# Masked attention stages: VectorE's minimum takes three heads of four, TensorE's penalties one, and the first unit's x leads the queue

## What is computed

```python
# stage 0 (L0)
attn = jnp.einsum('bnhd,bmhd->bhnm', q, k) * scale
attn = jnp.where(xa_mask[:, None, :, :], neg, attn)
attn = jax.nn.softmax(attn, axis=-1)
out = jnp.einsum('bhnm,bmhd->bnhd', attn, v).reshape(B, N, C)
x = x + (out @ proj_w + proj_b)
h = layer_norm(x, n2_w, n2_b)
x = x + jax.nn.gelu(h @ fc1_w + fc1_b) @ fc2_w + fc2_b
# stage 2 (L1, self-attention)
scores = jnp.where(mask[None, None], -jnp.inf, scores)
```

## Time and profile before

| | us |
|---|---|
| median of 3 runs | 5056.27 (5054.94 to 5061.84) |
| profiled execution | 5050.86 |
| its span, first to last instruction | 5049.1 |
| mean granted TensorE clock | 0.980 of full speed |

### The profile page before, as it was taken

How to read it: one execution, slowest core, us unless ns; L and a number is a source line. 1 busy time by engine, 2 the same in 40 slices (tenths; PEclk the granted TensorE clock), 3 DMA queues, 4 the chain that set the end, 5 groups by cost and what they waited for, 6 DMA issues and landing times.

```text
span 5049.1 us, 66199 instructions
## 1 busy us (share of the span) xinstructions
PE 4650.1 (92%) x24484; PEld 1878.1 (37%) x24484; DVE 3031.1 (60%) x7970; ACT 2308.9 (46%) x3011; POOL 968.6 (19%) x831
## 2 busy tenths in 40 slices
PE   6899999889998999999899988899889999999999
PEld 2333333333333333343444433333333333333333
DVE  5777776556777777666466675455534455545554
ACT  3455554456664444434455554444443333333332
POOL 0111111101110111111111111111113343333333
PEclk9999999999999999999999999999999999999999
DMA  1111111121121110001211211111120000000000
GB/s 57 37 44 58 48 41 44 35 78 64 58 65 52 35 39 32 31 30 44 70 63 59 68 62 49 37 37 34 39 76 21 10 3 13 13 13 13 1 13 9
DMA packets 152306, 201.55 MB, mean 40 GB/s; under 512 B 18993, under 2 KB 102321, under 8 KB 150706
## 3 DMA queue, kind: packets, MB, share of 16 engines
q1 hardware_dynamic: 151986, 197.31, 11.7%
HBM read 128.86 MB, written 68.42 MB: 39 GB/s over the span
## 4 chain that ended last, share of the span: by engine, by line
PE 59%; issue 18%; DVE 15%; ACT 4%; DMA 3%; POOL 1%; SPq 0%; DVEq 0%; POOLq 0%; ACTq 0%
PE psO L720 8%; PE small L649 7%; PE small L656 6%; PE psT L695 5%; PE psT L925 5%; PE psS L677 4%; DVE nmb L1169 4%; PE psT L778 3%; PE psT L649 2%; PE psT L885 2%; PE psO L940 2%; PE psT L895 2%; PE psT L940 2%; DVE nmb L1166 2%; DVE xn L1146 2%
## 5 line engine op out<-in xcount | busy, mean ns | idle before, releaser
L989 ACT ACTIVATE probs<-psT 128x1024 f32<-128x1024 f32 (+3 forms) x1280 | 1160.3, 961 | 1262.3 <-PE psT L695 1091.0
L1169 DVE TENSOR_REDUCE nmb<-psS 128x1 bf16<-128x512 f32 x1024 | 649.2, 685 | 279.2 <-PE psS L677 279.1
L1166 DVE CUSTOM_DVE_ANT_0 out<-psS,pens_sb 128x512 f32<-128x512 f32 x1024 | 665.7, 686 | 242.3 <-issue 241.1
L695 PE MATMUL psT<-low 32*128 32x512 f32 (+3 forms) x5120 | 750.0, 604 | 27.9 <-ACT probs L989 24.5
L677 PE MATMUL psS<-out 32*128 32x512 bf16 (+3 forms) x2560 | 592.6, 376 | 104.2 <-DVE nmb L1166 49.9
L720 PE MATMUL psO<-probs,V 128*32 128x512 f32 (+3 forms) x5120 | 658.1, 586 | 28.2 <-DVE probs L1178 26.6
L1352 DVE TENSOR_REDUCE parts<-psS 128x2 bf16<-128x1024 f32 x256 | 315.0, 1230 | 531.1 <-PE psS L912 531.1
L1095 ACT ACTIVATE probs<-psT 128x1024 f32<-128x1024 f32 x256 | 262.2, 1024 | 524.8 <-PE psT L928 524.8
L677 PEld LDWEIGHTS psS<-out 32*128 32x128 bf16 x2560 | 148.5, 91 | 800.8 <-issue 439.2
L778 PE MATMUL psT<-out,W 128*128 128x512 f32 x768 | 382.8, 620 | 0.4
L1019 ACT ACTIVATE low<-small,vec 128x256 f32<-128x256 f32 (+1 forms) x464 | 262.3, 618 | 231.7 <-PE small L649 231.7
(11 more groups left out here) (177 smaller groups left out, 5659.1 us busy)
## 6 DMA issues: line engine op xcount, KB each, us to landing
o_mid<-out SPq DMA_DIRECT2D x160, 256.0 KB, 2.0
oN<-o_mid SPq DMA_DIRECT2D x160, 128.0 KB
oN<-r_mid SPq DMA_DIRECT2D x80, 256.0 KB
x_mid<-xe SPq DMA_DIRECT2D x40, 512.0 KB, 2.9
xw<-x_mid SPq DMA_DIRECT2D x36, 512.0 KB, 4.1
xe<-x_mid SPq DMA_DIRECT2D x36, 512.0 KB, 5.0
cT<-ctxT SPq DMA_DIRECT2D x20, 512.0 KB, 7.5
W<-wm SPq DMA_DIRECT2D x6, 1024.0 KB, 7.8
```

Source lines behind the costliest of these rows:

```text
L695: last = nc.tensor.matmul(psT[j][:, q0:S], Kf[rows_of(j), q, a, c, kt * P:(kt + 1) * P], Qf[rows_of(j), q, a, c, q0:S], start=True, stop=p ...
L989: nc.scalar.activation(probs[:, i % 2, two, q0:S], psT_all[:, two, q0:S], ACT.Exp, scale=float(DH) ** -0.5)\
L1166: nc.vector.tensor_tensor_reduce(junk[:, e, 0:n], psS[e][:, 0:n], penalty, 1.0, -3.0e38, ALU.add, ALU.max, at).then_inc(sem[f"s_read{e}"], 1)
L1169: nc.vector.tensor_reduce(at, psS[e][:, 0:n], AX, ALU.max).then_inc(sem[f"s_read{e}"], 1)
```

## The change

In masked stages VectorE's minimum takes heads 1, 2 and 3 (128 x 1536 in one instruction) and so waits for both exponentials of the step. TensorE adds a penalty only to head 0; the matmul of head 0's penalty now counts `st_full` for heads 0 and 1. At the start SP issues x of the first unit ahead of Wqkv, and Wo, W1, W2 behind the first body's loads; TensorE waits for W1 and W2 only behind the first unit's body.

```diff
@@ body of SP @@
                     sp.dma_start(xw[:], src).then_inc(sem["x_in"], 16)
+                    if cur is None:
+                        sp.dma_start(Wqkv[:], wa[0, :, 0:N_QKV]).then_inc(qkv_in, 16)
@@ start of SP @@
-            sp.dma_start(Wqkv[:], wa[0, :, 0:N_QKV]).then_inc(qkv_in, 16)
-            sp.dma_start(Wo[:], wa[0, :, N_QKV:]).then_inc(wo_in, 16)
-            sp.dma_start(W1[:], wm1[0]).then_inc(wm_in, 16)
-            sp.dma_start(W2[:], wm2[0]).then_inc(wm_in, 16)
             for n, _ in enumerate(walk(sp, body)):
                 s, kind = divmod(n - 1, 3)
+                if n == 0:
+                    sp.dma_start(Wo[:], wa[0, :, N_QKV:]).then_inc(wo_in, 16)
+                    sp.dma_start(W1[:], wm1[0]).then_inc(wm_in, 16)
+                    sp.dma_start(W2[:], wm2[0]).then_inc(wm_in, 16)
@@ exp_scores @@
-                    plain = u.s != CAUSAL and not (u.s in MASKED and j < 2)
+                    plain = u.s != CAUSAL and not (u.s in MASKED and j == 0)
...
-                    if plain and j % 2:
+                    if plain and j % 2 and not (u.s in MASKED and j == 1):
                         last.then_inc(sem["st_full"], 1)
-                for j in range(2 if u.s in MASKED else 4 if u.s == CAUSAL else 0):
+                for j in range(1 if u.s in MASKED else 4 if u.s == CAUSAL else 0):
...
-                    if j % 2:
+                    if j % 2 or u.s in MASKED:
                         last.then_inc(sem["st_full"], 1)
@@ TensorE's program @@
-            pe.wait_ge(wm_in, 32)
             for n, _ in enumerate(walk(pe, body)):
                 s, kind = divmod(n - 1, 3)
+                if n == 1:
+                    pe.wait_ge(wm_in, 32)
@@ limit @@
-                dve.wait_ge(sem["exp_done"], count("exp_done", u, 2 * i + 1))
+                dve.wait_ge(sem["exp_done"], count("exp_done", u, 2 * i + 2))
...
-                two, row = probs[:, i % 2, 2:4, :], masking(lims, u)[:, i % T * S:(i % T + 1) * S]
-                both = bass.AP(tensor=row.tensor, offset=row.offset, ap=[list(row.ap[0]), [0, 2], list(row.ap[1])])
-                nc.vector.tensor_tensor(two, two, both, ALU.min).then_inc(sem["limited"], 1)
+                three, row = probs[:, i % 2, 1:4, :], masking(lims, u)[:, i % T * S:(i % T + 1) * S]
+                limits = bass.AP(tensor=row.tensor, offset=row.offset, ap=[list(row.ap[0]), [0, 3], list(row.ap[1])])
+                nc.vector.tensor_tensor(three, three, limits, ALU.min).then_inc(sem["limited"], 1)
```

## The result

The changed kernel takes 5134.0 us as median (5124.0 to 5145.4, 4 runs), the kernel before 5059.1 beside it (5054.9 to 5067.8, 4 runs): 1.0145 times as long, 95% interval 1.0125 to 1.0166. The forecast was 5088, 5050 to 5125. The direction was right, the size wrong: +75 us, not +32.

The account below looks back on a forecast made before the run. TensorE was busy 92%, but VectorE set some stretches of a unit. First units 2 x 5.5, steady units 7 x 1.8 and 7 x 2.0, less 6 at the start: +32 on the median 5056.27, 5088 us; range 5050 to 5125.

Parts of the forecast that it names:

- the start: First loads: with 2.5 MB of weights no longer ahead of x and masks, gain 6 us, between 3 and 8.
- the savings: TensorE's dropped penalty matmuls: 0.22 us each, ceiling 56 us; mostly waited away, 0.9 counted in each first unit.
- the last stretch: End of a steady unit, from VectorE's wait at 697.63: five savings of -1.1 waited away again, 0.0 in sum.
- The minimum's price: VectorE's minimum over 512 more columns: 0.53 us more, about 1.75 in all; 136 us over 256 minima.
- The later wait: The minimum waits for both exponentials: costed at nothing, covered by 2.8 us; without cover 0.96 each, 21 us in all.
- A unit's first stretch: Steady unit from 613.17, VectorE running through: outputs +1.06, then +1.59; the unit goes on at +1.06.
- the walk: Step-by-step count of a steady unit: +1.8 us in stage 0, about +2.0 in stage 2; as walked 5088, chance 0.58.
- Rival D: TensorE's clock falls in the new gaps, one more drop a unit: +24 us, 5112; chance 0.10.
- The stretch before the MLP: Steady unit from 635.88: four longer minima against 1.35 us of slack, outputs at 651.54 come +0.77 later.
- B: Rival: VectorE's slack suffices, only the first stretch pays; -0.9 us a steady unit, first units covered: 5037; chance 0.12.
- C: Rival between: steady units gain 0.9 us each, first units at +5.5 each: 5048, the same; chance 0.15.
- The first units: Each masked stage's first unit, without MLP: about 12 of 16 steps take the whole 0.53, less 0.9: +5.5, twice.

Follow-up runs that it names:

- e4_wait: e1_queue with one line changed: the minimum of two heads waits for both exponentials; 5056.15 us, 0.9978 of the kernel before.
- e1_queue: The kernel before with only the new order of the first loads; 5054.58 us, 0.9982 of the kernel before.
- e3_keep: The changed kernel with TensorE still adding penalties to heads 0 and 1; three-head minimum, later wait and new load order stay; 5114.11 us, 1.0096 of before.
- h3_three: e1_queue with the minimum taking three heads, with the later wait and one penalty, in steps 3, 9 and 10 only; 5082.05 us, 1.0023 of before.
- e5_drop: e1_queue with head 1's penalty dropped, that head left unmasked and the minimum kept at two heads; 5060.82 us, 0.9988 of before.
- h4_both: e1_queue with one-head minimum, three penalties behind the scores: all steps of masked stages' first units, seven steps of other units; 5032.45 us, 0.9925 of before.
- f1_fill: The changed kernel with matmuls of zeros into psO ahead of the wait for the minimum in steps 1, 2, 6, 11, 13; 5130.43 us, 1.0123 of before.
- g1_one: e1_queue with the minimum taking one head in every masked step, TensorE adding three penalties, one between the score pairs; 5335.64 us, 1.0528 of before.
- h2_one: e1_queue with the minimum taking one head in all masked steps, three penalties placed behind the four heads' scores; 5035.48 us, 0.9938 of before.

## Why the prediction was right or wrong

By the runs alone, in the prediction's terms: the start was put at -6 and gave -10 (between -2.5 and -16); the longer minima without the savings were put at some +39 (14 units at +1.8 to +2.0, two first ones at 6.4) and cost +58; the dropped penalties were put at -1.8 in all (0.9 in each first unit) and cost +20 to +25. The two steps that failed are the last stretch of the steady unit, put at 0.0, and the clock, put at nothing in the sum.

**The minimum's price: right.** 0.53 was taken between 0.47 and 0.61. The median went from 1.218 to 1.749 us, and VectorE's busy time in the masked stages by 130 us against 136.

**The later wait: right.** 22 waits became 29, and e4_wait can't be told from e1_queue.

**The start: right.** x reached VectorE at 6.79 (7 was said), the masks ScalarE at 12.21 (12), and hT came at 15.83 (16):

```profile
6.79 1.40 DVE L1123 BATCH_NORM_STATS2 stats<-xw 128x6 f32<-128x256 f32 x4
...
12.21 1.91 ACT L1030 ACTIVATE pens_sb<-out 128x2048 bf16<-128x2048 uint8 x1 [7.29 <-DMA out<-maskBT]
...
15.83 0.76 ACT L1014 ACTIVATE hT<-small,vec 128x512 f32<-128x512 f32 x1
```

The first minimum is 6.7 us earlier, against 6; e1_queue's median is 9.8 less.

**A unit's first stretch: the mechanism right.** The walk had the first outputs at +1.06 and the second at +1.59. The unit of the changed kernel from 746.46, against the earlier trace rows:

```profile
753.30 1.06 PE L722 MATMUL psO<-probs,V 128*32 128x512 f32 x8 [1.28 <-DVE probs L1181]
...
757.41 0.66 PE L646 MATMUL small<-ident,xn 128*128 128x128 f32 x4 [1.39 <-DVE xn L1149]
...
759.57 1.94 PE L722 MATMUL psO<-probs,V 128*32 128x512 f32 x8 [1.51 <-DVE probs L1181]
761.44 1.12 PE L646 MATMUL small<-ident,xn 128*128 128x128 f32 x4
```

Relative to the unit's first minimum the outputs of 753.30 are +1.06, those of 759.57 +1.59. In a unit at full clock (e3_keep) they are the same within 0.01, and +0.8 is left at the projection where +1.06 was walked.

**The step that failed first: the clock, left out of the sum, and the dropped penalties, counted as a saving or nothing.** In the rows above, behind three waits of 1.28, 1.39 and 1.51 us, outputs that take 1.06 take 1.94, and transposes that take 0.66 take 1.12: TensorE at 1.2 instead of 2.4 GHz. In the changed kernel such drops lie mostly in steps 1 and 2 and in 10 to 12, behind waits for minima and maxima. It is tempting to say that the longer waits made them. e3_keep says that they are not enough. The same stretch of its unit from 629.51, with two penalties a step and nearly the same waits (1.18 us for the second instead of 1.39):

```profile
636.35 1.07 PE L722 MATMUL psO<-probs,V 128*32 128x512 f32 x8 [1.28 <-DVE probs L1181]
...
640.47 0.65 PE L646 MATMUL small<-ident,xn 128*128 128x128 f32 x4 [1.18 <-DVE xn L1149]
...
642.63 1.06 PE L722 MATMUL psO<-probs,V 128*32 128x512 f32 x8 [1.51 <-DVE probs L1181]
643.63 0.66 PE L646 MATMUL small<-ident,xn 128*128 128x128 f32 x4
```

Most other units of e3_keep do have one drop, as those of the kernel before do; over both stages it is 72 us at half clock against the changed kernel's 188. So what the sum lacked is a price in clock for the work taken off TensorE, higher where it waits more. Rival D had the clock, at 0.10 and +24 for "one more such drop a unit", but as an alternative to the walk and for the gaps alone. It was an addition to the walk, and some 35 to 40 us by both prices (20 to 25 in the runs, net of what the dropped matmuls are worth at equal clock): 116 us over 16 units is 7.3 us a unit at half clock, 2.2 to 2.5 us of time against the 1.5 of D's drop. The Trainium skill, "TensorE: Matmul & The Clock Gate", section "HAM oscillation — how this bites in real kernels", tells of a kernel whose repeated waits put the clock back each time. The runs agree with it only in part: e3_keep has the longer waits at the clock of before, and in h3_three 48 matmuls fewer, behind minima that are hidden, came to +20 us. Its case waits for DMAs for longer than any of the three waits above, and a unit here is TensorE-busy for over 90%.

**The term that was mis-sized: the last stretch.** Walked 0.0, measured +1.5 (three outputs of +0.53 each, in e3_keep and the changed kernel alike). The unit that was walked holds a half-clock drop just there, the 2.31 us of the earlier trace rows; it slowed TensorE and so gave VectorE room that e1_queue's unit at full clock does not have, 1.39 us at 708.52:

```profile
708.52 0.69 DVE L1166 CUSTOM_DVE_ANT_0 out<-psS,pens_sb 128x512 f32<-128x512 f32 x1 [1.39 <-issue]
...
714.09 0.42 DVE L1195 COPY V<-small 128x256 f32<-128x256 f32 x1 [0.15 <-PE small L656]
...
717.12 0.69 DVE L1166 CUSTOM_DVE_ANT_0 out<-psS,pens_sb 128x512 f32<-128x512 f32 x1 [0.24 <-issue]
```

That hid the first of the three. The other two could be read here: behind the drop VectorE idles 0.15 and 0.24 us in steps to which a minimum adds 0.53, so that the walk's own remark, that VectorE runs through almost without idle time, speaks against its 0.0. Without the drop VectorE sets the pace over steps 12 to 14. In e3_keep, where nothing is dropped, the unit came to +0.8, +0.74 and +1.5, +3.04 in all; in the changed kernel, without its drops, to +2.4 to +2.9 instead of +1.8 and +2.0, 7 to 14 us in all. The stretch before the MLP, walked at +0.77, came to +0.74 in e3_keep.

**The savings.** The walk took the dropped penalties of the steady units as waited away, which was nearly right at equal clock (0.9 of 3.5 us a unit remained in e5_drop), and let 0.9 stand in each first unit; B and C counted 2 us a unit. No term allowed for a loss. e5_drop shows that the clock takes the gain back, and the changed kernel against e3_keep that it takes 20 to 25 us more.

**The first units.** Walked +5.5 each, measured +10.1 and +11.5, with 20 us more at half clock in each. Some +3 to +5 of it is the walk's term, by 0.30 to 0.35 for each us, and the rest the clock. e3_keep's first unit of stage 2 gives the term directly: +5.2 over e1_queue's with the same 6.8 us at half clock, where the walk has 6.4 without the savings.

**Rivals B and C: wrong.** TensorE's idle time in a unit did not stay near 6 us (111.87 us against 101.10 busy in the unit at 746.46). C's 5048 also lies just outside the range that was said to take it in.

**The signs that were named.** The minimum at 1.75: yes. Waits for minima two to three times as long: 1.7 times, the rest of the waiting being for maxima. A steady unit of stage 0 at 111 us: 112.4 as mean of units 1 to 7 (892.51 less 105.74, by 7), against 109.3. "A lower granted clock in the masked stages (D)" was named as a sign of error, and is what came. "Unmasked stages and the tail unchanged": what follows stage 2 took 18.5 us longer in the profiled execution, at 147 us of half clock against 102. h4_both, the fastest kernel, shows the same there, 2658.5 us at 143, and f1_fill 2641.3 at 106; with the same code it follows the clock of the execution, not the change. That is part of why the spans differ by 88 us and the medians by 75.

**What stays open.** Whether filled gaps could give the changed kernel its 35 us back: f1_fill moved the clock but not, measurably, the time, and other placings weren't tried. Nor is it known why nearly the same waits leave the clock alone with one more penalty a step; the runs show that they do. What sets the drops behind stage 2 from one execution to the next wasn't tried either.

## What to carry to other kernels

A matmul taken from an engine that already waits is worth little (0.9 of 3.5 us a unit here), and where the granted clock already drops now and then it can be worth less than nothing: cost the clock as an addition to every walk that takes work off TensorE, above all where its waits get longer too, and not as a rival to it. Walk a unit whose granted clock is 1.00 throughout, or correct for its drops, since a drop in the reference unit can hide which engine sets the pace. When a trade between two engines loses at equal clock, try it in the other direction in the steps where the paying engine is the bound: here one head instead of three for VectorE in the right steps gave 0.9925 with the new queue order, which gave 0.9982 by itself.

## What the runs showed of the hardware

Four matmuls on 32 rows each of the array run together in 1.14 to 1.24 us only while nothing stands between them. One 128-row penalty between the two pairs made each pair take 1.13. Over g1_one that brought the scores' busy time, 741.5 us in h2_one, to this row of its page. Against h2_one it cost 300 us, 1.17 us in each of 256 steps, a part of which is clock (mean 0.971 against 0.983):

```profile
L704 PE MATMUL psT<-low 32*128 32x512 f32 (+3 forms) x5120 | 1021.1, 608 | 56.9 <-issue 28.4
```

And less work can lengthen busy time: TensorE was busy 1593.3 us in the masked stages before and 1599.8 after, with 56 us of penalties removed: 116 us more of the time was at 1.2 GHz, where matmuls that take 1.06 us take 1.94. And longer waits alone did not lower the clock: e3_keep, with TensorE's waits for minima at 44.5 us instead of 26.7 and its work as before, has its runs at 0.976 to 0.979, e1_queue at 0.974 to 0.982.
